# Gathers in three lots with waits of their own, and LSTM input products for four steps at once

## The reference

```python
x = x + _L0_conv_ref(_gn(x), ...)   # block attention with a halo, 4 heads
x = x + _L1_conv_ref(_gn(x), ...)   # LSTM along the width, hidden size 128, then a linear map
x = x + _L2_conv_ref(_gn(x), ...)   # deformable 3x3 convolution
x = x + _L3_conv_ref(_gn(x), M)     # 8x8 block transform
```

```python
x_gates = jnp.einsum('ntc,gc->ntg', y, W_ih) + b_ih + b_hh
g = xg + h @ W_hh.T
i, f, gg, o = jnp.split(g, 4, axis=-1)
c = jax.nn.sigmoid(f) * c + jax.nn.sigmoid(i) * jnp.tanh(gg)
h = jax.nn.sigmoid(o) * jnp.tanh(c)
```

## Time and profile before

| | us |
|---|---|
| median of 3 runs (lowest, highest) | 3991.52 (3990.05, 3993.2) |
| profiled execution: its own time | 3983.06 |
| profiled execution: span from first to last instruction | 3981.3 |
| POOL busy in it | 2632.5 (66%) |
| PE busy | 2310.4 (58%) |
| DVE busy | 2114.3 (53%) |
| ACT busy | 1085.6 (27%) |

### The profile page before, as it was taken

How to read it: one execution, slowest core, us unless ns; L and a number is a source line. 1 busy time by engine, 2 the same in 40 slices (tenths; PEclk the granted TensorE clock), 3 DMA queues, 4 the chain that set the end, 5 groups by cost and what they waited for, 6 DMA issues and landing times.

```text
span 3981.3 us, 52655 instructions
## 1 busy us (share of the span) xinstructions
PE 2310.4 (58%) x19558; PEld 1853.3 (47%) x19558; DVE 2114.3 (53%) x4326; ACT 1085.6 (27%) x2728; POOL 2632.5 (66%) x2614
## 2 busy tenths in 40 slices
PE   6879967876877577767764576677773120101112
PEld 4667744655766355556663355466652120101112
DVE  5754467865555786655455776565455332222222
ACT  4554434423223243232231343232221000000000
POOL 1000047777777777777777777777777777777775
PEclk9889977876676777677677677677676555555555
DMA  7510036733113465331123555331131221111111
GB/s 244 177 48 22 1 116 197 206 84 93 51 51 107 129 189 161 90 93 51 52 67 102 161 162 169 81 80 53 52 116 54 71 64 52 52 53 52 52 52 49
DMA packets 185056, 373.94 MB, mean 94 GB/s; under 512 B 59368, under 2 KB 89320, under 8 KB 183616
## 3 DMA queue, kind: packets, MB, share of 16 engines
q1 hardware_dynamic: 100848, 200.11, 16.4%
q0 software_dynamic: 82944, 170.04, 16.2%
q10 hardware_dynamic: 1008, 0.43, 0.0%
HBM read 265.15 MB, written 104.33 MB: 93 GB/s over the span
## 4 chain that ended last, share of the span: by engine, by line
POOL 60%; issue 19%; DVE 2%; PE 2%; DMA 1%; ACT 0%; SPq 0%; POOLq 0%; DVEq 0%; ACTq 0%
POOL got L598 60%; PE gates L1489 1%; DVE mx L979 0%; DMA got<-sample_table,index 0%; PE bank L1295 0%; DVE got L884 0%; DMA qst<-mparts 0%; DVE red L889 0%; PE gates L1479 0%; PE gates L1623 0%; PE bank L1358 0%; DVE sums_in L1005 0%; PE gates L1375 0%; DMA qst<-q_parts 0%; DVE prod L1149 0%
## 5 line engine op out<-in xcount | busy, mean ns | idle before, releaser
L598 POOL DMA_INDIRECT got<-sample_table,index x2592 | 2619.1, 1010 | 1268.7 <-issue 787.2
L884 DVE TENSOR_TENSOR got<-got,weight 128x1152 f32<-128x1152 f32 x288 | 392.9, 1364 | 975.8 <-DMA got<-sample_table,index 975.5
L1295 PE MATMUL bank<-turned,wout 128*128 128x96 f32 x1728 | 317.1, 362 | 779.3 <-DVE x L905 532.8
L1295 PEld LDWEIGHTS bank<-turned,wout 128*128 128x128 f32 x1728 | 304.8, 274 | 796.5 <-DVE turned L899 717.9
L1489 PE MATMUL gates<-hist,whh 128*128 128x96 f32 x2280 | 447.0, 360 | 220.0 <-DVE hist L1155 218.8
L1489 PEld LDWEIGHTS gates<-hist,whh 128*128 128x128 f32 x2280 | 402.3, 265 | 270.6 <-DVE hist L1155 269.6
L979 DVE TENSOR_REDUCE mx<-gates 128x2 f32<-128x392 f32 x576 | 296.0, 554 | 95.4 <-PE gates L1375 92.5
L676 ACT ACTIVATE pt<-gates 98x512 f32<-98x512 f32 x384 | 217.9, 594 | 314.1 <-PE gates L1389 313.2
L1375 PE MATMUL gates<-kst,qst 96*128 96x196 bf16 x1152 | 192.1, 288 | 164.8 <-DVE mx L979 130.3
L616 ACT ACTIVATE std<-bank,eps 128x1 f32<-128x1 f32 x16 | 4.2, 261 | 958.3 <-PE bank L1285 958.3
L1406 PE MATMUL bank<-pt,v 98*18 98x128 f32 x4608 | 215.2, 312 | 67.1 <-issue 66.1
(11 more groups left out here) (156 smaller groups left out, 3910.0 us busy)
## 6 DMA issues: line engine op xcount, KB each, us to landing
kst<-k_parts SPq DMA_DIRECT2D x96, 441.0 KB
got<-sample_table,index POOLq DMA_INDIRECT x2592
qst<-q_parts SPq DMA_DIRECT2D x96, 288.0 KB
k_parts<-kp SPq DMA_DIRECT2D x24, 882.0 KB
k_parts<-kp SPq DMA_DIRECT2D x24, 588.0 KB
q_parts<-qp SPq DMA_DIRECT2D x24, 576.0 KB
q_parts<-qp SPq DMA_DIRECT2D x24, 384.0 KB
k_parts<-kp SPq DMA_DIRECT2D x24, 294.0 KB
```

Of the source, the lines that this page charges most:

```text
L598: pool.indirect_dma_start(out=got[:, uu % RING, n, :], out_offset=None, in_=tables[p], in_offset=bass.IndirectOffsetOnAxis(ap=at, axis=0)) ...
L884: dve.tensor_tensor(corners, corners, w, ALU.mult).then_inc(weighted, 1)
L1295: mm = pe.matmul(out_ps[n % 2][:, at:at + GN], wout[:, tap, :], turned[:, k % 2, tap, :], start=(tap == 0), stop=(tap == NTAP - 1))
```

## The change

Two edits. First, POOL's wait for `reduced` stays before a unit's first gather; before the fourth gather a wait for `summed` of the unit six before is added, and before the seventh a wait for `weighted` of the unit five before. Second, in images 1 to 3 the input products are made for four steps at once: a gate takes 384 columns of its bank, `ones` is twice as wide, and the 12 matmuls have 384 columns and stand after every fourth step.

```diff
+FOUR = 4
+KH = 3
...
-            ones = sb("ones", [96, 2 * W], BF16, where=a1)
+            ones = sb("ones", [96, FOUR * W], BF16, where=a1)
...
-        gate = [bank[1 + n][:, 0:2 * W] for n in range(4)]
+        gate = [bank[1 + n][:, 0:FOUR * W] for n in range(4)]
...
-                    wait(pool, reduced, uu - RING + 1)
-                    pool.sem_inc(pool_passed, 1)
                     for n in range(NTAP):
+                        if n == 0:
+                            wait(pool, reduced, uu - RING + 1)
+                            pool.sem_inc(pool_passed, 1)
+                        if n == KH:
+                            wait(pool, summed, uu - RING + 1)
+                        if n == 2 * KH:
+                            wait(pool, weighted, uu - RING + 2)
...
+                        h = W * (t % FOUR)
                         act.wait_ge(g_done, tt + 1)
...
-                    xin = xs[:, :, first:first + 2, :].rearrange("p j t f -> p t j f")
-                    for n, g in enumerate(BOTH_GATE_OF):
+                    xin = xs[:, :, first:first + FOUR, :].rearrange("p j t f -> p t j f")
+                    for n, g in enumerate(FOUR_GATE_OF):
...
-                    h = W * (t % 2)
-                    for n, g in enumerate(BOTH_GATE_OF):
+                    h = W * (t % FOUR)
+                    for n, g in enumerate(FOUR_GATE_OF):
...
-                            both_recurrence(t)
-                        if t % 2 == 1 and t + 1 < W:
-                            both_inputs(t + 1)
+                            four_recurrence(t)
+                        if t % FOUR == FOUR - 1 and t + 1 < W:
+                            four_inputs(t + 1)
```

More of the change, by code:

```diff
@@ L46 @@
 LIN = 8
+FOUR = 4
 GATE_OF = (1, 2, 0, 3)
-BOTH_GATE_OF = (2, 0, 1, 3)
+FOUR_GATE_OF = (2, 0, 1, 3)
 WARM = 4
@@ L1469, in lstm, with four_inputs @@
             def lstm(p):
-                def both_inputs(first):
+                def four_inputs(first):
                     for k, (begin, _) in enumerate(CHUNKS):
@@ L1483, in both_inputs, with four_recurrence @@
                             mm.then_inc((g_done, None, if_done, o_done)[n], 1)
-                def both_recurrence(t):
+                def four_recurrence(t):
                     pe.wait_ge(hid_done, W * p + t)
-                    h = W * (t % 2)
-                    for n, g in enumerate(BOTH_GATE_OF):
+                    h = W * (t % FOUR)
+                    for n, g in enumerate(FOUR_GATE_OF):
                         mm = pe.matmul(gate[n][:, h:h + W], whh[:, HID * g:HID * (g + 1)], hist[:, (t - 1) % HIST, :], start=False, stop=True,
@@ L1547, in lstm @@
                 else:
-                    both_inputs(0)
+                    four_inputs(0)
                 for t in range(W):
```

## The result

The changed kernel takes 3997.68 us (median of 20 runs, 3989.0 to 4007.49), the kernel before 3984.45 in the 20 runs beside it (3972.11 to 3993.2). The ratio is 1.0033 with a 95% interval of 1.0024 to 1.0042: slower by 13 us, 10 to 17. The prediction had 16 us and 4007.5; it started from the median of the first three runs, 3991.52, which lay high among the 20.

A forecast was written before the change was run, and what follows sets the result against it. POOL's gather issue was taken as the bound: 541.6 us before the first gather, 3408.8 + 16.0 of gathers and 31.1 behind them made a 3997.5 span; 16.2 above the 3991.52 median was given as 4007.5 us, range 4000 to 4018.

The forecast's parts named there:

- The three terms: Whole span: 541.4 us before the first gather, 2592 gathers on POOL without a hole, 31.1 us behind them.
- Part 1, waits at 0: POOL's list: 564 added waits, whose conditions are already met, cost 0, at most 23 us.
- Part 2, the steps: LSTM, images 1 to 3: merged products save nothing and hide less; four steps go from 13.4 to 14.4 us.
- Part 2, the late units: LSTM stages, images 1 to 3: DVE catches up more slowly, so 28 more units reach `weigh` after their gathers landed.
- The price: Gathers stretched by a `weigh` that DVE reaches late: 0.57 us per such unit, 28 x 0.57 = 16.0 us.
- No change: Whole kernel stays at 3991.7 us, by exclusive port locking or a higher clock more often; chance 0.31.
- Faster through the higher clock: LSTM stages: long product runs bring TensorE's higher clock for good, 9 us won, 3983; chance 0.06.
- Costly waits: POOL's list: added waits lengthen pauses to 0.34 us, 23 us, total 4030 or 4015; chance 0.05.
- All units late: Three LSTM stages: DVE misses all 57 landings it had waited for, 32 us, total 4024; chance 0.10.
- The lock rule: DVE and GpSimd ports: the first holds the lock for its instruction; late `weigh` costs no extra, four-step products cost 0.

The follow-up runs named there:

- run 10: Kernel before with `weigh`, `halve`, the first add of `turn` and attention's four k and q subtractions each cut into three instructions: 3893.41 us, ratio 0.9754.
- run 1: Kernel before with only the added waits of POOL, before the fourth and seventh gathers: 4028.66 us, ratio 0.9997.
- run 2: Kernel before with only the input products of four steps at once, POOL's list as before: 4034.76 us, ratio 1.0013.
- run 3: The changed kernel again, beside the kernel before in another set: 4040.55 against 4030.55 us, ratio 1.0033.
- run 4: Kernel before with one more unused tanh of ACT in each LSTM step of images 1 to 3: 4044.19 us, ratio 1.0035.
- run 5: Kernel before with three more unused tanh of ACT in each LSTM step of images 1 to 3: 4066.1 us, ratio 1.0087.
- run 8: Kernel before with `weigh` cut into three instructions of three taps, each behind the end of the one before: 3924.86 us, ratio 0.9838.
- run 9: The changed kernel with `weigh` cut into three instructions, against the kernel before: 3928.55 us, ratio 0.984.
- run 6: Kernel before with the input products of one step (12 matmuls of 96 columns) after each step: 4038.29 us, ratio 1.0014.
- run 12: Kernel before with a one-column memset and a wait for its end ahead of `weigh`: 3987.6 us, ratio 0.9986.

## Why the prediction was right

**The three terms.** The time is still the start of the gathers, their sum and the tail. The tail is 31.0 us (3956.9 to 3987.9) against the 31.1 of before. The start moved by 3.3 in the profiled executions and by chance.

In all profiles here but run 10's the pauses are 789 to 790 us and the tail is 30 to 32, so what a kernel gains or loses lies in the length of its gathers or in where the first one begins.

**Part 1, waits at 0.** Shown: run 1 has ratio 1.000 with an upper end of 6 us, and pauses of 0.305 us everywhere.

**Part 2, the steps.** 2.69 us of products were to show in one step of four at the lower clock, 2.64 did; products 0.32 apart were expected, 0.317 found; the mean clock stayed at 0.71. Four steps without a wait for a gather took 13.9 us on average before and 14.7 after, where 13.4 and 14.4 were worked out; the working left out the convolutions that stand in some steps. These terms are right.

**Part 2, the late units.** 28 more were predicted; waits fell by 19. The mis-sized term is image 1: it was to use all its 31 units to catch up and none would wait, but 8 did, at a granted clock of 0.70 against its 0.68 before. Images 2 and 3 lost 7 and 8 waits, 15, nearly as worked out (8 and 8).

**The price.** 0.57 us each was the middle of 0.47 and 0.66. The traces give it unit by unit, if the excess over 0.94 us of each gather that ends 0.82 us behind a `weigh` is put down to that unit. For the 95 units of the three stages:

| kernel | waiting, late | us for a waiting one | us for a late one | `weigh`'s sum | all stretches there |
|---|---|---|---|---|---|
| before | 57, 38 | 0.15 | 0.51 | 28.1 | 53.4 |
| changed | 38, 57 | 0.10 | 0.58 | 37.0 | 62.7 |
| run 1 (waits alone) | 50, 45 | 0.45 | 0.56 | 47.8 | 72.1 |
| run 2 (four steps alone) | 44, 51 | 0.34 | 0.60 | 45.3 | 71.6 |
| run 3 (changed again) | 43, 52 | 0.41 | 0.59 | 48.1 | 76.4 |
| run 4 (one tanh) | 52, 43 | 0.27 | 0.70 | 44.0 | 76.6 |
| run 5 (three tanh) | 0, 95 | | 0.69 | 65.1 | 92.7 |
| run 8 (thirds) | 27, 68 | 0.02 | 0.11 | 8.0 | 32.5 |
| run 9 (thirds, changed) | 2, 93 | 0.00 | 0.14 | 12.8 | 38.8 |

In the first comparison the stages hold 9.3 us more of stretches, and 8.9 of them are at `weigh`: 8.9 / 19 = 0.47 us for each unit that became late. That is the mechanism of the prediction, at the lower of its two prices. 28 x 0.57 = 16 came out as 19 x 0.47 = 9 in the stages, and as 13 (10 to 17) in the medians. That 16 lies so near to 13 is in part luck: both factors were too high, and 4 us of the 13 are found in no row.

**How far this is shown.** Runs 8 and 9 differ by the change alone, and with `weigh` in thirds its cost is less than 13 us; their traces have 25 more late units and 4.8 us more at `weigh`. So a part of the change's cost goes through the long `weigh` of late units. That this is all of it is not shown. Where waiting units are caught too, a late one costs only 0.1 to 0.3 us more than a waiting one (runs 1 to 3), 7 units are all that separate runs 1 and 3, and the ratio is 1.0033 nevertheless; and run 4 cost 14 us with no more late units than run 1. A changed step also shifts the other DVE instructions against the gathers, and the count of waiting `weigh` is not the whole of the price.

**The rivals.** No change: excluded by the interval. Faster through the higher clock: the long run of products did bring the higher clock, but for about two steps and not for good, and the mean did not move; run 6 shows that it can move (0.60). Costly waits: excluded by run 1. All units late: 38 still waited; run 5 shows the case at 35 us, where 32 were given, but only 17 of them at `weigh` in the stages. The lock rule of the Trainium skill, "SBUF — State Buffer", section on who interferes with whom, holds in one direction only: a gather waits for a DVE instruction with two SBUF inputs that began before it got its turn (2.12 us), a DVE instruction that begins inside a gather does not wait for it (0.95 and 1.36 us side by side, and again in run 12; of the 1942 `weigh` that began less than 0.85 us into a gather or up to 0.03 us ahead of it the longest took 1.42 us).

**Where it was off.** The scatter: I took 0.1% from three runs, and 20 have a range of 0.5% (3972 to 3993).

## What to carry to other kernels

Where one engine's list of short DMA issues is the bound, look at the distribution of the issue's own time, not only at waits: 0.94 against 2.12 us told here which work on another engine mattered, and cutting that work into pieces, each of which waits for the one before, gave 2.5%, while edits that only moved hidden work gave 0.3% the wrong way. Work off the path can still cost through when it starts. And the matmuls here, bound by their columns, gained nothing from being merged, and lost the cover that lay between them. A count that rests on one trace of each kernel (57, 50; 38, 43) is weaker than a ratio of medians: size an effect by both.

## What the runs showed of the hardware

- **An edge of a few hundredths of a us.** A `weigh` that began 0.05 us before a gather cost it 1.17 us; one that began 0.1 or 0.2 us behind it cost it nothing and the next one 0.16. Whether a landing falls on one side or the other differs between sets of runs of the same kernel (27 us in the last part alone).
- **Not every DVE instruction holds a gather up.** In the traces of before, after and runs 1, 3 and 4, of the gathers that began inside a DVE instruction with at least 0.25 us of it to come, those inside `weigh` (634), `halve` (277), the first add of `turn` (70) and `prod` (29) all ended 0.82 us behind it; all have two SBUF inputs. Of those inside `mx<-gates` (489, its input in PSUM), the reciprocal (163) and the transpose of `turn` (101) none did.
- **A gather gets in between two DVE instructions where the second waits for the first.** The gather behind the first of three thirds took 1.33 us.
- **The granted clock differed with the shape of TensorE's work:** 0.72 with 12 products of 384 columns after every fourth step, 0.71 with 192 after every second, 0.60 with 96 after each, with the same columns in all. With 384 it mostly rose by the end of the products' run (55 of 69), and in 41 of 72 cases it was down again, in part at least, two steps later.
